# Splitting x into its four phases by strided copies instead of two transposes, with ScalarE taking the convolution out of PSUM

## The reference

```python
out = conv1d(x, weight, groups=4, K=9, pad=4)        # 32 channels in, 32 out
out = out + (c @ c_weight.T)[:, :, None] + bias[None, :, None]   # context: one number per sample and channel
logits = out @ W_gate + b_gate                       # 512 -> 8 experts, per row
top_idx = top_k(logits, 2)
y_all = relu(out @ W_e + b_e)                        # 8 experts, 512 -> 512
x = x + mean(y_all[chosen two])
```

## Time and profile before

| what | value |
|---|---|
| median of 3 runs | 514.61 us (514.56 to 514.78) |
| the profiled execution | 515.17 us |
| its span, first to last instruction | 513.4 us |
| PE busy, share of the span | 496.1 us, 97% |
| DVE busy | 347.0 us, 68% |
| ACT busy | 121.0 us, 24% |
| POOL busy | 153.3 us, 30% |
| mean granted TensorE clock | 0.995 of full speed |

### The profile page before, as it was taken

The page is one execution under the profiler, slowest core; times in us unless marked ns, Lnnn a source line. Parts: engine busy times, 40 slices in busy tenths (PEclk is TensorE's granted clock), DMA queues, the critical chain, the costliest instruction groups (busy, mean ns, idle before and its releaser), DMA issues. The chain is left out here.

```text
span 513.4 us, 10342 instructions
## 1 busy us (share of the span) xinstructions
PE 496.1 (97%) x2412; PEld 329.5 (64%) x2413; DVE 347.0 (68%) x1082; ACT 121.0 (24%) x277; POOL 153.3 (30%) x178
## 2 busy tenths in 40 slices
PE   6999999999999999999999999999997999999996
PEld 5999999999964444444444444444544676767674
DVE  4588888888866547573354445444445899999996
ACT  3232333334421111111111111111123222222220
POOL 9144444444447322233323323332224000000000
PEclk9999999999998999999999999999999999999999
DMA  4969978999885686676665767675554798888852
GB/s 111 290 216 291 274 270 287 324 364 324 235 220 165 200 229 156 166 203 172 176 176 162 184 163 200 163 188 158 150 147 141 252 343 278 288 284 281 296 180 102
DMA packets 91442, 113.07 MB, mean 220 GB/s; under 512 B 25438, under 2 KB 62222, under 8 KB 90372
## 3 DMA queue, kind: packets, MB, share of 16 engines
q1 hardware_dynamic: 73200, 71.26, 49.3%
q0 software_dynamic: 11664, 36.24, 19.3%
q10 hardware_dynamic: 6536, 5.10, 3.5%
HBM read 67.55 MB, written 46.52 MB: 222 GB/s over the span
## 5 line engine op out<-in xcount | busy, mean ns | idle before, releaser
L1196 PE MATMUL bank<-we,lT 128*128 x536 | 233.6, 597 | 1.7 <-DVE ring_a L935 1.6
L1196 PEld LDWEIGHTS bank<-we,lT 128*128 128x128 f32 x536 | 101.7, 191 | 129.0 <-issue 128.8
L935 DVE TENSOR_TENSOR ring_a<-bank,be_bc 128x512 f32<-128x512 f32 x71 | 48.9, 690 | 104.4 <-PE bank L1196 50.4
L541 POOL DMA_INDIRECT pairs_d<-ring_b,pair_i x71 | 71.1, 1002 | 161.3 <-DVE pair_i L924 113.7
L1169 PE MATMUL bank<-wconv,phases 128*128 128x128 f32 x768 | 91.8, 276 | 0.7 <-ACT phases L567 0.7
L620 ACT ACTIVATE ring_b<-ring_a 128x512 f32<-128x512 f32 x71 | 44.7, 631 | 196.7 <-DVE ring_a L935 181.5
L1169 PEld LDWEIGHTS bank<-wconv,phases 128*128 128x128 f32 x768 | 89.1, 193 | 0.9 <-ACT phases L567 0.9
L524 POOL DMA_INDIRECT lists_d<-token_list,row_i x64 | 62.9, 983 | 83.6 <-DVE row_i L845 50.1
L921 DVE STREAM_TRANSPOSE lT<-xt 128x512 f32<-128x512 f32 x71 | 49.8, 702 | 5.7 <-DMA keys<-lists_d 5.4
L1263 PE MATMUL bank<-wq,high 128*128 128x512 f32 x128 | 37.4, 414 | 3.4 <-PEq L1211 3.4
L1157 PE MATMUL bank<-wg,lT 128*128 128x136 f32 x256 | 37.4, 289 | 1.1 <-DVE partial L816 1.1
(11 more groups left out here) (194 smaller groups left out, 401.4 us busy)
## 6 DMA issues: line engine op xcount, KB each, us to landing
xt<-lists_d SPq DMA_DIRECT2D x284, 64.0 KB
xt<-in_x SPq DMA_DIRECT2D x60, 256.0 KB, 4.1
we<-pairs_d SPq DMA_DIRECT2D x28, 512.0 KB, 4.8
we<-in_L_ffn_W_e SPq DMA_DIRECT2D x8, 1024.0 KB
out<-orow_list SPq DMA_DIRECT2D x32, 256.0 KB, 2.8
lists_d<-orow_list SPq DMA_DIRECT2D x8, 257.0 KB
be_bc<-in_L_ffn_b_e ACTq DMA_DIRECT2D x4, 512.0 KB
words<-pairs_d POOLq DMA_DIRECT2D x4, 512.0 KB, 5.4
```

The costliest lines, as they stand in the source:

```text
L541: pool.indirect_dma_start(pairs_d, bass.IndirectOffsetOnAxis(ap=pair_i[:, s % DR:s % DR + 1], axis=0), ring_b[:, s % U, :], None, bounds_c ...
L935: dve.tensor_tensor(ring_a[:, j % 2, :], ps_exp[j % 2][:, :], be_bc[:, bass.ds(expert, 1), :].rearrange("p a n -> p (a n)"), ALU.add).then ...
L1196: mm = pe.matmul(ps_exp[j % 2][:, :], lT[:, j, p * P:(p + 1) * P], we[:, bass.ds(expert, 1), p, :].rearrange("m a n -> m (a n)"), start=(p ...
```

## The change

The phases are no longer made by transposes. SP loads each group of x on 32 partitions only, as channel x (sample, position): `x_quad[j]` is quarter j of the partitions of `xt`, over all four slots. Each phase is then one copy of 32 x 512 elements with a source step of 4 elements (16 bytes), from the group's quarter to the phase's quarter of `phases`: phases 0 and 1 on DVE (`split_x`), 2 and 3 on ACT. ACT, not DVE, takes the convolution out of its bank. The context leaves `hT`: ACT adds it as a bias per row (`ctx_col`) in the copy to `token_list`, and DVE adds a table `gate_bias` (context times the column sums of the gate's weights, plus b_gate) to the logits instead of b_gate. The round trip of the context through HBM and its broadcasts are gone. The loads of the start are reordered, and of two groups of 8 warm-up transposes one stays, ahead of everything. Nothing of stages 2 and 3 is edited, but SP's list loads wait for other semaphores.

```diff
+        def split_phase(copy, q, jq, jb):
+            return copy(phases[q * C:(q + 1) * C, jb, :, 1:P + 1],
+                        x_quad[jq].rearrange("c s (l q) -> c q s l", q=PH)[:, q, :, :])
...
 # SP
+            sp.dma_start(x_quad[0], x_sub[0]).then_inc(x_in[0], 16)
+            sp.wait_ge(wfull_zero, 1)
+            for s in range(2):       # the other two of conv_w: on ACT's queue
+                sp.dma_start(wfull[rows, rows, PH - 1:PH - 1 + TAPS], conv_w[rows]).then_inc(convw_in, 16)
...
-                    sp.wait_ge(xT_ready, k * XR + j + 1)
-                    sp.dma_start(xt[:, j, :], x_g[...]).then_inc(x_in[j], 16)
+                    sp.wait_ge(act_split, k * XR + j + 1)
+                    sp.wait_ge(dve_split, k * XR + j + 1)
+                    sp.dma_start(x_quad[j], x_sub[...]).then_inc(x_in[j], 16)
...
                     if isinstance(a, int) and a < XR:
-                        sp.wait_ge(xT_ready, NG - XR + a + 1)
+                        sp.wait_ge(act_split, NG)
+                        sp.wait_ge(dve_split, NG)
...
 # ACT, step g
-                    act.copy(phases[...], ps_ph[...]).then_inc(ph_ready, 1)
+                    wait(act, conv_done, g + 1)
+                    wait(act, tok_done, g - 1)
+                    act.copy(hT[...], ps_conv[j % 2][...]).then_inc(hT_ready, 1)
+                    wait(act, x_in[ja], ring_count(a, ja, XR))       # a = g + 2
+                    wait(act, conv_done, a - 1)
+                    for q in range(PH // 2, PH):
+                        ins = split_phase(act.copy, q, ja, j % 2)
+                    ins.then_inc(act_split, 1)
...
-                        ins = act.copy(rows[:, b, :, :, :], ps_both[...])
+                        ins = act.activation(rows[:, b, :, :, :], ps_both[...], ACT.Identity, bias=ctx_col[:, bass.ds(a, 1)])
...
 # DVE
-                dve.transpose(ring_a[...], xt[:, ja, :].rearrange("c (h l q) -> c q h l", h=MH, q=PH)).then_inc(xT_ready, 1)
+                for q in range(PH // 2):
+                    ins = split_phase(dve.tensor_copy, q, ja, ja % 2)
+                ins.then_inc(dve_split, 1)
...
-                    dve.tensor_tensor(hT[...], ps_conv[j % 2][...], ctx_bc[...], ALU.add).then_inc(hT_ready, 1)
...
-                    dve.tensor_tensor(logit[:, :], partial[:, :], bg_bc[:, :], ALU.add)
+                    dve.tensor_tensor(logit[:, :], partial[:, :], gate_bias[...], ALU.add)
...
 # PE
-            def transpose_phases(a, ja):
-                wait(pe, xT_ready, a + 1)
-                wait(pe, ph_ready, a)
-                for h in range(MH):
-                    mm = pe.transpose(ps_ph[:, h * P:(h + 1) * P], ring_a[...], ident[:, :])
-                mm.then_inc(ph_done, 1)
...
-            transpose_phases(0, 0)
-            warm_up(WARM_START)
+            def context_products():       # once, behind the convolution of group 0
+                pe.matmul(ps_misc[:, 0:N], cwT[...], condT[:, :], start=True, stop=True).then_inc(ctx_mm, 1)
+                for p in range(PH):
+                    mm = pe.matmul(bank[0][:, 0:E], one_row[:, 0:1].to_broadcast((P, P)), wg[:, p, 0:E], ...)
+                mm.then_inc(gate_sum, 1)
...
                 if live(g, NG):
-                    wait(pe, ph_ready, g + 1)
+                    wait(pe, act_split, g + 1)
+                    wait(pe, dve_split, g + 1)
...
-                if live(g + 1, NG):
-                    transpose_phases(g + 1, j + 1)
```

More of the change, by code:

```diff
@@ L116, in build_program @@
         xt = sb("xt", [P, XR, L])
+        x_quad = [xt[i * C:(i + 1) * C, :, :] for i in range(XR)]
         ring_a = sb("ring_a", [P, 2, L])
@@ L554, in _ @@
         def _(act):
-            act.dma_start(fs_bc[:, :], fside.rearrange("(a c) -> a c", a=1).to_broadcast((P, C))).then_inc(fs_in, 16)
+            act.wait_ge(wfull_zero, 1)
+            for s in range(2, C // CG):
+                rows = slice(s * CG, (s + 1) * CG)
+                act.dma_start(wfull[rows, rows, PH - 1:PH - 1 + TAPS], conv_w[rows]).then_inc(convw_in, 16)
+            act.dma_start(bg_bc[:, :], b_gate.rearrange("(a e) -> a e", a=1).to_broadcast((P, E))).then_inc(bg_in, 16)
             act.wait_ge(ident_ready, 2)
@@ L608, in _ @@
             act.wait_ge(pads_ready, 2)
[L609 removed]
+            stepped(act, step1, -2, lo1, hi1, NG + 2)
             act.wait_ge(mlp_mm, 7)
@@ L770, in rank_split, with context_columns @@
                 deq_step(dve.scalar_tensor_tensor(terms_w[:, :], full_low, odd[0:RK, 0:1], full, ALU.mult, ALU.add))
-            transpose_x(1, 1)
+            split_x(1, 1)
             dve.wait_ge(consts, N_CONSTS)
-            dve.wait_ge(bg_in, 16)
+            def context_columns():
+                dve.wait_ge(ctx_mm, 1)
+                dve.wait_ge(fs_in, 16 * SUB)
+                for s in range(SUB):
+                    rows = slice(s * C, (s + 1) * C)
+                    dve.tensor_scalar(ctx_col[rows, :], ps_misc[rows, 0:N].rearrange("p (g s) -> p s g", s=SUB)[:, s, :],
+                                      fs_col[rows, 0:1], None, ALU.add).then_inc(ctx_ready, 1)
+                dve.wait_ge(gate_sum, 1)
+                dve.wait_ge(ctx_ready, SUB)
+                dve.tensor_tensor(gate_bias[:, :, :], ctx_col[:, :].rearrange("p (g a) -> p g a", a=1).to_broadcast((P, NG, E)),
+                                  bank[0][:, 0:E].rearrange("p (a e) -> p a e", a=1).to_broadcast((P, NG, E)), ALU.mult).then_inc(gbias_ready, 1)
+                dve.wait_ge(gbias_ready, 1)
+                dve.wait_ge(bg_in, 16)
+                dve.tensor_tensor(gate_bias[:, :, :], gate_bias[:, :, :],
+                                  bg_bc[:, :].rearrange("p (a e) -> p a e", a=1).to_broadcast((P, NG, E)), ALU.add).then_inc(gbias_ready, 1)
             def mix_softmax(step):
```

112 lines of the change are left out of this document (47 added, 65 removed).

## The result

The changed kernel takes 517.93 us (median of 12 runs, 516.45 to 519.70); the kernel before, beside it, 515.46 (12 runs, 513.93 to 518.08). The ratio is 1.0046, with an interval of 1.0027 to 1.0065: **slower by about 2.4 us** (0.5%, small but clear of noise), where 11 us less were forecast. The profiled execution took 518.35 us, its span is 516.6 and its granted clock 0.981 on average (before: 515.17, 513.4, 0.995).

The account below looks back on a forecast made before the run. PE's weight loads were taken to bound stage 1. Start -1.9, 27 periods -11.9, end of stage 1 +2.1 and clock +0.8 gave -10.9: 515.17 to 504.3, as median 503.7 us; 8-in-10 range 499.5 to 512.0.

Parts of the forecast that it names:

- The transposes go: 0.44 less on PE, period 3.73, if nobody else is late: Stage 1: PE's period falls from 4.17 to 3.73 us; over 27 periods, 11.9 us less.
- DVE starts the logits 0.38 after the gate's last load and ends `chosen` 1.93 later: DVE's chain in each stage 1 group: `chosen` at T + 3.43, T being the end of a convolution's loads.
- The sum from T + 0.31 is T + 3.98, but successive instructions overlap by 0.10: ACT's step per group ends at T + 3.48, 0.38 us before the gate wants the bank at T + 3.86.
- with the bias taken as free: ACT's two row copies per group: 0.38 us each, adding the context as bias costs nothing.
- ACT's rival: ACT bounds stage 1 with strided copies of 1.40 us: period 4.03, gain 3.8 instead of 11.9, 511.8 us; chance 0.17.
- DVE's copies: DVE's two strided phase copies per group take 0.65 us each; up to 0.745 each costs nothing.
- the rival at 1.04: DVE bounds stage 1 with copies of 1.04 us: period 4.32, 4.1 us more instead of 11.9 less, 519.7; chance 0.15.
- The start: Up to the end of convolution 2: at 21.1 us instead of 22.96, 1.9 us less (0.5 to 3).
- I add 0.9: Convolution of group 0 pays 0.9 us for missing warm-ups on its loads, so it ends at 13.5.
- The end of stage 1: List 0 waits for group 31's splits; PE waits 3.6 us, product 0 at T + 14.2, 2.1 us more.
- I add half, 0.8 us: PE's idle 3.6 us at the end of stage 1 may lower its clock: half of 1.6 us added.
- without the wait it would be T + 10.5, 1.6 less: End of stage 1 without list 0's added wait: product 0 at T + 10.5 instead of T + 12.07.

Follow-up runs that it names:

- e5: Changed kernel with lists 0 and 1 of stage 2 loaded early into ring_a and DVE's loop written out: 509.48 us, 0.9885 of the kernel before.
- e8: Changed kernel with lists early, DVE's loop written out, be_bc loaded early, ACT's phase copies contiguous (wrong elements): 504.74 us, 0.9802 of the kernel before.
- e6: Changed kernel with lists 0 and 1 early and be_bc loaded in groups 0 to 3: 510.03 us, 0.9894 of the kernel before.
- e12: Changed kernel with lists early, be_bc loaded early and ACT's phase copies contiguous (wrong elements): 509.04 us, 0.9868 of the kernel before.
- e2: Changed kernel with ACT's two phase copies reading contiguous elements (phases 2 and 3 wrong): 515.80 us, 1.0018 of the kernel before.
- e9: Changed kernel with lists early, DVE's loop written out and be_bc loaded early, nothing left out: 509.66 us, 0.9875 of the kernel before.
- e1: Changed kernel with lists 0 and 1 of stage 2 loaded into ring_a, without waiting for group 31's splits: 509.93 us, 0.9897 of the kernel before.
- e10: Kernel before the change with only DVE's loop over groups 4 to 15 written out: 513.23 us, 0.9962 of the kernel before.
- e14: As e9, with POOL's memset of mix_bd moved behind the last scatter: 511.35 us, 0.9934 of the kernel before.

## Why the prediction was wrong, step by step

**The step that failed** is "The transposes go: 0.44 less on PE, period 3.73, if nobody else is late", times 27. It brought 2.1 us, not 11.9. By stretch, forecast and measured: periods 0 and 1, -0.9 and +0.2; the loop, -5.3 and -2.1; periods 14 to 19, -2.6 and -1.7; the last seven, -3.1 and +1.4. Three things were late, one behind the other:
- DVE in the loop. "DVE starts the logits 0.38 after the gate's last load and ends `chosen` 1.93 later" was read from one group outside the loop and used for the 12 periods inside. No rival had it: DVE's was priced on the copies alone. In the loop the chain is 2.75. With 1.28 for the copies that makes 4.03, and the loop ran at 4.07. The 4.25 a period in the loop before, against the 4.17 of that group, was a sign of it. Written out, the loop ran at 3.98 (e5), and e8, with ACT and transfers eased, at 3.87.
- ACT outside the loop. "The sum from T + 0.31 is T + 3.98, but successive instructions overlap by 0.10" gave T + 3.48. Measured are 1.16 and 1.13 from start to start for the strided copies (forecast 0.96) and 0.94 for the row copies (0.56, "with the bias taken as free"). Together with L568 and the keys that is 3.94, T + 4.25 against the T + 3.86 that the gate allows. So ACT's rival came true in these periods (4.03 there, 3.90 here). Its price, 3.8 us less for the 27 periods, assumed nothing else.
- The last seven periods. Transfers at a share of 1.03 around 100 us, two ACT_TABLE_LOADs of 1.28 each (before under ACT's idle time, now in a step without any), and the layers behind them. This stretch is slower than before the change, which no case had. e6 and e12 show the transfers' part (1.2 us alone, 3.3 with the copies eased). The table loads' part is not measured by itself; the last of these periods takes 5.84 us (4.50 before), and in it PE waits for the layer behind the second table load:

```profile
131.76 0.08 PEld L1149 LDWEIGHTS bank<-ident,att_n 128*8 128x8 f32 x1 [1.02 <-DVE att_n L812]
```

**DVE's copies** were forecast well: 0.62 each for 0.65, and the rival at 1.04 didn't come. **What a step of 16 bytes costs** differs by engine: on ACT 0.50 us (1117 ns against 616 contiguous, e2), on DVE 0.2 at most (623 ns, inside the 427 to 639 of the contiguous rows, which are casts of another tile; no run makes the same copy contiguous on DVE). So the rule of the Trainium skill (SBUF — State Buffer, the note on cachelines), that each crossing to a new 16-byte line pays, agrees with ACT's rows, and DVE's rows leave it open. The prediction weighed it for DVE alone.

**The start**: 0.4 less at the end of convolution 2 (22.96 to 22.55), forecast 1.9. Convolution 0 starts 0.5 later (9.74 for 9.2), and its loads take 5.20, where "I add 0.9" left 4.3 (9.2 to 13.5): the two make up the 1.5. DVE's copies behind POOL's memset cost nothing here, since they end at 16.09 and convolution 1 starts at 16.26, right behind the context products; only where convolution 0 is quicker, as in e9, do they show.

**The end of stage 1**: the mechanism held (DVE 5.18 for 5, PE 3.73 for 3.6). The wait by itself was sized well: 2.1 and 1.6 make 3.7, and of the 5.5 us that e1 gives back ahead of product 0 two are the half speed of two gates, which leaves 3.5. Two terms were wrong. The clock's was too small: "I add half, 0.8 us", and it was 3.6, 2.0 in the gates and 1.6 in product 0. And "without the wait it would be T + 10.5, 1.6 less" brought 0.1: e1 has 11.47 us where before had 11.60.

**The sum**: -0.85 - 2.1 + 5.33 + 0.82 = +3.2, the difference of the two profiled executions; the medians differ by 2.5. Not settled are what makes the clock fall in one execution and not in the next, all of e10's gain, the slower runs of e14, and the table loads' part.

## What to carry to other kernels

When the engine that sets the pace is relieved by 10%, read the step of every other engine as a sum from start to start, in each form in which the step exists (in a loop, written out, at the end): a chain measured in one form isn't that of the other. Work moved to an idle engine also takes the cover from what was hidden there, such as waits for scatters. And limits of nearly the same length hide each other, so test them in combinations: here three edits worth 0, 1 and 1 us alone in the 27 periods gave 7.8 together.

A buffer that is laid out anew changes when its slots come free. The one wait that this added cost more (7 us) than all that the change gained (3), and a spare buffer took it away.

Before a difference of one or two microseconds is given to an edit, compare the granted clock of the two executions in the stretches that the edit doesn't touch.

## What the hardware showed that I had not expected

- A copy of 32x512 f32 with a step of 16 bytes: ACT 1117 ns, contiguous 616; DVE 623.
- The same DVE instructions of the changed kernel, `partial` to `chosen`: 2.04 us written out, 2.75 in a loop with registers.
- One DVE copy beside a POOL memset of 3.53 us took 5.49 us, and two such copies 1.23 once the memset was away.
- With PE standing from 142.8 us, the granted clock fell to 0.50 (1.2 GHz) at about 145 and rose at about 155, with PE busy from 146.5 for most of it. It also fell with PE busy for 10 us on end: before at 160, in e14 at 153.
- The same wait of 3.5 us ahead of stage 3 was followed by 6 to 7 us at half speed in some profiled executions (after, e9) and by none in others (before, e1).
- At the start 24 weight loads took 3.5 to 5.2 us, where later ones take 2.76, with a granted clock of 1.00 in the rows.
- A POOL copy that is made to wait for the scatter ahead of it waited 6.57 us for its landing.
